# Two layers of a graph network with routed experts: an earlier release of the expert operands in layer 0, and a front of layer 1 that requests its rows itself and lets GpSimd add them

## What is computed

```python
# end of layer 0: the experts
logits = xn @ Wr + br
top_vals, top_idx = top_k(logits, 2)
w = softmax(top_vals)
for e in range(8):
    h = gelu(xn @ W1[e] + b1[e])
    y_e = h @ W2[e] + b2[e]
    y += y_e * w_full[e]
x = x + y
# start of layer 1: the "front"
xn = layernorm(x)
xw = xn @ W                      # for the graph convolution
q = xn @ Wq; k, v = xn @ Wkv     # for linear attention: elu(q)+1, elu(k)+1
context = sum over nodes of k (x) v
```

## Time and profile before

| what | value |
|---|---|
| three runs of the kernel | 2505.94, 2511.72, 2512.45 us (median 2511.72) |
| the profiled execution, its own time | 2507.24 us |
| its span, first to last instruction | 2505.5 us |
| PE, DVE, ACT, POOL busy | 80%, 61%, 41%, 18% of the span |
| mean granted TensorE clock | 0.896 |
| layer 0's experts: first gather, last scatter issued | 955.8, 1218.2 us |
| layer 1's front: first to last of its instructions on DVE | 1244.2, 1391.6 us |

### The profile page before, as it was taken

The page is one execution under the profiler, slowest core; times in us unless marked ns, Lnnn a source line. Parts: engine busy times, 40 slices in busy tenths (PEclk is TensorE's granted clock), DMA queues, the critical chain, the costliest instruction groups (busy, mean ns, idle before and its releaser), DMA issues. The chain is left out here.

```text
span 2505.5 us, 41612 instructions
## 1 busy us (share of the span) xinstructions
PE 2007.9 (80%) x12047; PEld 1623.7 (65%) x12047; DVE 1516.8 (61%) x3970; ACT 1023.8 (41%) x1839; POOL 455.2 (18%) x478
## 2 busy tenths in 40 slices
PE   6948888788874247888388779868999975899998
PEld 4536666556532236777355567648888864899998
DVE  3479999788618773333255622249999947344443
ACT  3525555455300113555244134326666631333332
POOL 0000000166300003444100000000000000354443
PEclk9979999887895559999789889989999985999999
DMA  2023333500470331111500054302122045444232
GB/s 65 0 68 125 125 120 118 149 1 1 94 182 0 100 107 45 57 59 58 127 10 0 7 138 129 87 21 59 54 62 60 28 123 184 131 111 98 47 49 35
DMA packets 90491, 190.03 MB, mean 76 GB/s; under 512 B 13711, under 2 KB 58272, under 8 KB 90410
## 3 DMA queue, kind: packets, MB, share of 16 engines
q1 hardware_dynamic: 72746, 157.63, 21.9%
q0 software_dynamic: 17664, 31.47, 5.9%
HBM read 124.54 MB, written 64.52 MB: 75 GB/s over the span
## 5 line engine op out<-in xcount | busy, mean ns | idle before, releaser
L1950 PEld LDWEIGHTS experts_ps_h<-experts_xt,experts_up 128*128 128x128 f32 x2944 | 346.9, 194 | 56.0 <-issue 51.8
L1950 PE MATMUL experts_ps_h<-experts_xt,experts_up 128*128 128x128 f32 x2944 | 356.4, 278 | 31.9 <-ACT experts_xt L1984 31.7
L2555 PE MATMUL gat_ps_o<-Y,gat_prob_t 125*125 125x256 f32 x1250 | 274.0, 379 | 0.0
L2041 DVE COPY experts_up<-up 128x1024 f32 (+1 forms) x184 | 122.6, 696 | 237.9 <-ACT experts_hid L1994 167.5
L2555 PEld LDWEIGHTS gat_ps_o<-Y,gat_prob_t 125*125 125x125 f32 x1250 | 232.6, 188 | 33.8
L1202 PE MATMUL adj_ps_w<-adj_one_k,adj_one_s 128*125 128x500 bf16 x1000 | 178.2, 304 | 80.0 <-DVE adj_one_k L1133 56.6
L1962 PE MATMUL experts_ps_o<-experts_down,experts_hid 128*128 128x256 f32 x960 | 226.8, 379 | 0.3 <-ACT experts_hid L1994 0.3
L2009 ACT ACTIVATE experts_down<-down 128x1024 f32 (+1 forms) x120 | 138.8, 1156 | 166.8 <-DVE experts_out L2061 103.9
L1962 PEld LDWEIGHTS experts_ps_o<-experts_down,experts_hid 128*128 128x128 f32 x960 | 173.1, 190 | 19.3 <-issue 0.5
L1202 PEld LDWEIGHTS adj_ps_w<-adj_one_k,adj_one_s 128*125 128x125 bf16 x1000 | 97.8, 137 | 129.9 <-DVE adj_one_k L1133 61.1
L1909 POOL DMA_INDIRECT experts_rows<-expert_rows,slot_src x120 | 120.3, 1003 | 253.9 <-POOLq L1525 217.9
(11 more groups left out here) (363 smaller groups left out, 3773.2 us busy)
## 6 DMA issues: line engine op xcount, KB each, us to landing
adjacency<-adj_tile SPq DMA_DIRECT2D x25, 683.6 KB
adjacency_t<-adj_tile_t SPq DMA_DIRECT2D x25, 683.6 KB
adj_in<-adjacency_t SPq DMA_DIRECT2D x25, 683.6 KB
gcn_adj<-adjacency SPq DMA_DIRECT2D x25, 683.6 KB
cnt<-adjacency_t SPq DMA_DIRECT2D x25, 683.6 KB
up<-in_L_ffn_w SPq DMA_DIRECT2D x32, 512.0 KB
down<-in_L_ffn_w SPq DMA_DIRECT2D x16, 512.0 KB
expert_rows<-route_row SPq DMA_DIRECT2D x10, 560.0 KB
```

The source lines that it names most:

```text
L1950: last = nc.tensor.matmul(ps[:, h * 128:(h + 1) * 128], w[:, k * H + h * 128:k * H + (h + 1) * 128], xt[b][:, k, :], start=(k == 0), stop= ...
L2041: last = nc.vector.tensor_copy(ups[r % 2][n][:], X.ups[n][:, bass.ds(place, 1), :].rearrange("p e w -> p (e w)"))
L2555: last = nc.tensor.matmul(ps_o[b][0:ROWS, 0:C], prob_t[:, s * ROWS:(s + 1) * ROWS], K.Y[:, s, :], start=(s == 0), stop=(s == TILES - 1))
```

## The change

It has three parts.

1. In layer 0's experts the first of the two result instructions signals a new semaphore `o_used` when it has read the product in PSUM and the bias in `downs`. `copy_down(t+2)` on ScalarE and `down(t+2)` on TensorE wait for that signal in place of `out_ready`, and VectorE waits for it itself where it had a `drain`.
2. In the experts' block SP requests group 0's rows alone. The front requests the others: group 1 behind `wy` and `wkv`, then `wq`, then it waits for group 0, and then groups 2 to 4, of which each waits for the group two before it.
3. In the front VectorE adds the two parts for group 0 alone. For groups 1 to 4 GpSimd adds them, each ahead of the save of the group before; `statistics(g+1)` waits for it.

```diff
+def pair_rows(K, sp, g, sem):
+    tiles = slice(g * GROUP, (g + 1) * GROUP)
+    view = K.pair[0:2 * NODES].rearrange("(n t p) c -> n p t c", n=2, p=ROWS)
+    rows_dma(sp, K.XN[:, tiles, :], view[0, :, tiles, :], sem)
+    rows_dma(sp, K.Y[:, tiles, :], view[1, :, tiles, :], sem)
...
@@ front, sync: rows(g)
-                if x_landed is not None:
-                    sp.wait_ge(x_landed[g], 64)
-                    sp.nop().then_inc(x_in[g % 2], 32)
+                if g >= 2:
+                    sp.wait_ge(x_in[g % 2], g // 2 * x_full + START)
...
+                elif g:
+                    pair_rows(K, sp, g, x_in[g % 2])
                 else:
+                    sp.wait_ge(x_landed, x_full)
+                    sp.nop().then_inc(x_in[0], x_full)
...
             sp.dma_start(wkv[:], w_kv.rearrange("(k p) o -> p k o", p=128)).then_inc(w_in, 16)
-            if x_landed is None:
-                rows(1)
+            rows(1)
             sp.dma_start(wq[:], w_q.rearrange("(k p) o -> p k o", p=128)).then_inc(w_in, 16)
-            for g in range(2 if x_landed is None else 0, GROUPS):
+            if x_from is None:
+                rows(0)
+            for g in range(2, GROUPS):
                 rows(g)
@@ front, vector: statistics(g, b)
-                dve.wait_ge(x_in[b], (g - b) * 16 + 32 + START)
-                if x_landed is not None:
-                    tiles = bass.ds(g * GROUP, GROUP)
+                elif isinstance(g, int):
+                    dve.wait_ge(x_in[b], x_full + START)
                     for part in (K.XN, K.Y):
-                        nc.vector.tensor_tensor(K.X[:, tiles, :], K.X[:, tiles, :], part[:, tiles, :], ALU.add)
+                        nc.vector.tensor_tensor(K.X[:, 0:GROUP, :], K.X[:, 0:GROUP, :], part[:, 0:GROUP, :], ALU.add)
                         dve.drain()
+                else:
+                    dve.wait_ge(x_added, g * 2 + START)
@@ front, gpsimd
+            def add(g, b):
+                tiles = bass.ds(g * GROUP, GROUP)
+                pool.wait_ge(x_in[b], (g - b) * 32 + 64 + START)
+                nc.gpsimd.tensor_tensor(K.X[:, tiles, :], K.X[:, tiles, :], K.XN[:, tiles, :], ALU.add).then_inc(x_added, 1)
+                pool.wait_ge(x_added, g * 2 - 1 + START)
+                nc.gpsimd.tensor_tensor(K.X[:, tiles, :], K.X[:, tiles, :], K.Y[:, tiles, :], ALU.add).then_inc(x_added, 1)
...
+                for g in range(GROUPS):
+                    if g + 1 < GROUPS:
+                        add(g + 1, (g + 1) % 2)
+                    save(g)
@@ experts, sync
-                for g in range(GROUPS):
...
+                pair_rows(K, sp, 0, landed_x)
@@ experts, tensor: down(t)
-                    pe.wait_ge(out_ready, t - 1 + START)
+                    pe.wait_ge(o_used if L0 else out_ready, t - 1 + START)
@@ experts, scalar: copy_down(t)
                     if L0:
-                        act.wait_ge(out_ready, t - 1 + START)
+                        act.wait_ge(o_used, t - 1 + START)
@@ experts, vector: result(t)
-                    nc.vector.tensor_tensor(out[r % 4][:], ps_o[r % 2][:, 0:C], downs[r % 2][:, HB * C:], ALU.add)
-                    dve.drain()
+                    nc.vector.tensor_tensor(out[r % 4][:], ps_o[r % 2][:, 0:C], downs[r % 2][:, HB * C:],
+                                            ALU.add).then_inc(o_used, 1)
+                    dve.wait_ge(o_used, t + 1 + START)
                     nc.vector.tensor_scalar(out[r % 4][:], out[r % 4][:], share, None, ALU.mult).then_inc(out_ready, 1)
```

More of the change, by code:

```diff
@@ L269, in front @@
         x_in = [m.sem(f"x_in{i}") for i in range(2)]
-        deg_ready, deg_rooted = m.sem("deg_ready"), m.sem("deg_rooted")
+        deg_ready, deg_rooted, x_added = m.sem("deg_ready"), m.sem("deg_rooted"), m.sem("x_added")
+        x_full = 32 if x_landed is None else 64
         deg = m.sb("deg", (ROWS, TILES))
@@ L276, in rows @@
             def rows(g):
-                if x_landed is not None:
-                    sp.wait_ge(x_landed[g], 64)
-                    sp.nop().then_inc(x_in[g % 2], 32)
-                else:
[L281 to L285, removed]
-            if x_landed is None:
+                lo, tiles = g * GROUP, slice(g * GROUP, (g + 1) * GROUP)
+                if g >= 2:
+                    sp.wait_ge(x_in[g % 2], g // 2 * x_full + START)
+                if x_from is not None:
+                    rows_dma(sp, K.X[:, tiles, :],
+                             x_from[lo * ROWS:(lo + GROUP) * ROWS].rearrange("(t p) c -> p t c", p=ROWS), x_in[g % 2])
+                elif g:
+                    pair_rows(K, sp, g, x_in[g % 2])
+                else:
+                    sp.wait_ge(x_landed, x_full)
+                    sp.nop().then_inc(x_in[0], x_full)
+            if x_from is not None:
                 rows(0)
@@ L311, in statistics @@
             def statistics(g, b):
-                dve.wait_ge(x_in[b], (g - b) * 16 + 32 + START)
-                if x_landed is not None:
-                    tiles = bass.ds(g * GROUP, GROUP)
+                if x_from is not None:
+                    dve.wait_ge(x_in[b], (g - b) * 16 + 32 + START)
+                elif isinstance(g, int):
+                    dve.wait_ge(x_in[b], x_full + START)
                     for part in (K.XN, K.Y):
-                        nc.vector.tensor_tensor(K.X[:, tiles, :], K.X[:, tiles, :], part[:, tiles, :], ALU.add)
+                        nc.vector.tensor_tensor(K.X[:, 0:GROUP, :], K.X[:, 0:GROUP, :], part[:, 0:GROUP, :], ALU.add)
                         dve.drain()
+                else:
+                    dve.wait_ge(x_added, g * 2 + START)
                 layer_norm_stats(dve, nc, lambda u: K.X[:, g * GROUP + u, :], stats, mv, var_eps,
@@ L371, in _, with save @@
             K.banks.arm(pool, next_sems)
-            with pool.Fori(0, GROUPS) as g:
+            def save(g):
                 pool.wait_ge(xn_ready, g + 1 + START)
                 nc.gpsimd.tensor_copy(K.XN[:, bass.ds(g * GROUP, GROUP), :], xn[:]).then_inc(xn_saved, 1)
+            def add(g, b):
[4 more added lines that the diff above has]
+                nc.gpsimd.tensor_tensor(K.X[:, tiles, :], K.X[:, tiles, :], K.Y[:, tiles, :], ALU.add).then_inc(x_added, 1)
+            if x_from is not None:
+                with pool.Fori(0, GROUPS) as g:
+                    save(g)
+            else:
+                for g in range(GROUPS):
+                    if g + 1 < GROUPS:
+                        add(g + 1, (g + 1) % 2)
+                    save(g)
         @block.scalar
@@ L1867, in experts @@
         weights_in = [m.sem(f"weights_in{i}") for i in range(2)]
-        turned, xt_ready, h_done, h_ready, hid_ready, o_done, out_ready, out_free = (
-            m.sem(n) for n in ("turned", "xt_ready", "h_done", "h_ready", "hid_ready", "o_done", "out_ready", "out_free"))
+        turned, xt_ready, h_done, h_ready, hid_ready, o_done, o_used, out_ready, out_free = (
+            m.sem(n) for n in ("turned", "xt_ready", "h_done", "h_ready", "hid_ready", "o_done", "o_used", "out_ready",
+                               "out_free"))
         landed, up_copied, down_copied = (m.sem(n) for n in ("landed", "up_copied", "down_copied"))
@@ L2604, in program @@
             gin_up_tail(nc, K, D)
-        x_landed = K.banks.zero[24:24 + GROUPS]
+        x_landed = K.banks.zero[24]
         with ExitStack() as layer:
```

9 lines of the change are left out of this document (2 added, 7 removed).

## The result

| | before | after |
|---|---|---|
| median, us (4 runs each) | 2510.84 (2505.94 to 2512.45) | 2442.92 (2439.3 to 2444.78) |
| after / before | | 0.9731, 95% interval 0.9712 to 0.9749 |
| profiled execution, own time, us | 2507.24 | 2444.18 |
| its span, us | 2505.5 | 2442.5 |

A forecast was written before the change was run, and what follows sets the result against it. Stages separated by barriers were each judged by their last-ending wait: layer 0's experts' ring, the handover's weights, the front's keys. 26.5 + 17.0 + 12.6 + 4.4 = 60.5 us off 2507.24 gave 2446.7, forecast 2449 us, range 2438 to 2474.

The forecast's parts named there:

- Part 1: Layer 0's experts: the earlier signal removes 0.51 us from each of 53 steps, for a gain of 26.5 us.
- the ring: Layer 0's experts: Gelu, VectorE's copy, addition, gate product, ScalarE's copy, next Gelu set the step; 4.54 us becomes 4.03.
- The first rival: Layer 0's experts: VectorE's copy waits 0.59 us for GpSimd's gather in 48 steps; gain 36.5 us, 2473 us; chance 0.12.
- The cap: Layer 0's experts: TensorE needs 3.97 us a step, so the gain is at most 30.0 us.
- the sum: Whole kernel: 26.5 + 17.0 + 12.6 + 4.4 = 60.5 us off the profiled 2507.24, giving 2446.7 us.
- Part 2: Handover: with weights queued behind two groups instead of five, TensorE starts at about 1239.1 instead of 1256.05; 17.0 us gained.
- the bounds of 14.7 and 19: Handover gain: 14.7 us if SP stalls twice, 19 us if the weights slip in between rows.
- the forecast's 1231: Handover: estimated time when SP passes on group 0's rows after issuing `wq`, within 1228.4 to 1233.4.
- Part 3 and the clock: Front: moving additions to GpSimd returns 12.6 us of key waits; TensorE's clock no longer falling behind them gives 4.4 us.
- I charge nothing: Front: the fourth tile's key waits for GpSimd to about 1281.3, wanted at 1283.5; no cost, at worst 2 us.
- The reading of the saves: Front: GpSimd's pair for group g+2 starts behind group g's save, at 1278.0, and is wanted 15 us later.
- The median: Whole kernel: 2446.7 us plus half of the profiled execution's 4.5 us distance under its median gives 2449 us.

The follow-up runs named there:

- four buffers: The changed kernel with four buffers instead of two for layer 0's second matrix, so ScalarE's copy waits for tile t-4: 2429.17 us (0.9706 of before); again 2430.02 us (0.9717).
- the weights first: The changed kernel with `wq` requested ahead of group 1's rows in the handover: 2445.86 us (0.9771 of before).

## Why the prediction was right

- **Part 1, 26.5 us: right.** The stage gave 26.0, 26.2 alone, at 4.03 us a step. The product stands off the ring: 0.35 us more of it costs nothing in after and 15.1 us in before.
- **The first rival** (copy waits for gather) was answered by the step itself: copy 0.70 us, gather 1.21. By the rule of the Trainium skill (SBUF — State Buffer, "Who interferes with whom") the gather, which began first, would have kept the port for all of its time against a copy in a 2-port mode; in no step of after did it, and every copy took 0.69 to 0.72 us. The gather paid 0.24 us in most steps. That isn't a price of every overlap, though: with four buffers, where the gather begins 0.12 us ahead of the copy, both keep their times, 0.97 and 0.70 us. Why the one meeting stretches it and the other doesn't stays open.
- **The cap: wrong.** The step was "The cap is TensorE: 4.54 - 0.57 = 3.97 us a step against the ring's new 4.03, a gain of at most 30.0." The step with four buffers is 3.73 us, and the cap by it (4.54 - 3.73) x 54, some 44 us (the stage gave 41.6). This did not touch the sum, since the ring at 4.03 decided, but it hid a further 15 us. The 3.97 came from the idle time in front of TensorE's matmuls. The ends of these are modelled: the last matmul of the second product is drawn 0.38 us long although the next may begin 0.2 us after it, so the row counts as busy what is room. From the start of the second product to the next first product are 1.73 us with four buffers and 1.94 in after, where the row is drawn busy for 1.89 of them. Waits of the weight loads, in before over 965 to 1215 us, said more:

```profile
PEld experts_ps_h L1950 <- issue: 50.1, 54, 1.3
```

 That is 0.93 us a step in before and 0.42 in after. Taken off the step they give 3.61 in both, a little too low, as the matmul row is too high; 3.73 lies between, nearer to the second.
- **Part 2, 17.0 us: right**, 16.6, or 16.2 alone, and the bounds of 14.7 and 19 held. One error of detail cost nothing. VectorE started 1.6 us sooner than forecast: between the barrier and the end of `wq`'s request SP took 4.8 us, with one stall in them (a request of 1.96 us), where the forecast's 1231 stood for 6.9. The weights came as estimated, 21.2 us behind the last scatter where 20.9 was forecast, and they alone decided instead of together with the rows.
- **Part 3 and the clock, 12.6 + 4.4 = 17.0 us: right**, 17.8, or 17.1 alone. From a group's transposes to the key that was late, the four groups gave 3.47, 3.20, 3.19 and 3.20 us, 13.1 in all, where four waits of 3.24 or 3.11 are gone. From key to next transposes the four groups took 5.27, 4.21, 5.28 and 6.51 us before and 4.17, 4.10, 4.18 and 4.10 after, 4.7 us for the clock. That is all of the 17.8. (The waits in sum fell by 11.5 us only, 13.7 to 2.2, since after has short ones of its own in the second of these stretches.) GpSimd's addition, 3.0 us by estimate, took 2.88 to 3.08. The fourth tile's key was stretched as feared, and "I charge nothing" held for it. The reading of the saves was wrong: the one at 1276.75 in the earlier trace rows is group 1's, 21.23 us behind the end of group 0's, so group 2's pair comes a group earlier than forecast, right behind group 0's save and beside the first key. That cost 0.37 us in this trace, nothing in the one of after run again (the key 0.42 us, the wait 0.32), and more with the weights first, where the wait is 1.80.
- **The median: wrong in sign.** I added 2 us because the profiled execution of before lay below its median. The one of after lay above its own, so the medians are 67.9 us apart and the sum said 60.5. By the traces the three stages give 60.4, so the other 7.5 us of the medians' distance are no stage that the change touches. Run again beside nine runs of before on one chip, after was 58.7 us faster. So the sum, not the 67.9, is what the change is worth, and what put the forecast of the median 6 us too high is scatter of the runs.

Left open: why TensorE's clock comes up earlier in its work in one start of the front than in another, why a gather beside a copy is stretched in one kernel and not in another, and why the third interval of the front is 21.95 us where its neighbours have 21.15. None of them was tried.

## What to carry to other kernels

Before naming an engine as the next bound, give the ring one more buffer and run it: the idle time in front of matmuls understated TensorE's room by 0.24 us in a step of 4; the waits of its weight loads overstated it by 0.12 and were the better hint. Let a consumer be signalled by the instruction that last reads its buffer, not by the end of the group around it: 0.5 us a step, 54 times over. And where a transfer that an engine waits for is queued behind others that nobody wants yet, request it ahead of them; but look at what the earlier start meets.

## What the runs showed of the hardware

- TensorE ran in 190 us as many matmuls, some 1,330, as had shown it 99% busy over 205.
- A gather on GpSimd that began 0.4 us before a VectorE copy was stretched, 1.17 to 1.22 us in place of 0.97 in 42 of after's steps, and the copy kept its 0.70. One that began 0.12 us before the copy, with four buffers, kept its 0.97, and the copy its 0.70.
- A VectorE instruction with two SBUF inputs beside GpSimd's addition of 1280 elements took 2.25 and 2.32 us in place of 0.41.
- Two products of VectorE of 0.35 us, the second on the same input, follow each other by 0.27 us.
- Behind waits of TensorE of 3 us in the front its granted clock fell to 0.50 in some groups and not in others of the same kernel (6.51 and 4.21 us from key to transposes in before), and for the same group in one kernel and not in another (26.76 and 24.46 us). Behind waits of 0.69 us or less in after it did not, nor behind the one of 1.80 us with the weights first.
